# Attention products of two units issued together in one accumulator bank, with two buffers of transposed probabilities

## The reference, cut to what matters

```
h = ln(x) + shift;  qkv = h @ Wqkv.T
q, k = ln(q), ln(k)                        # per head
scores = q @ k.T / 8                       # [256, 256] per head
attn = softmax(scores);  o = attn @ v
x = x + o @ Wout.T
gate = softmax(x @ Wgate.T); each expert takes its 512 best tokens,
    applies ln, fc1, gelu, fc2, weights the result and adds it to its tokens
```

## Time and profile before

| | |
|---|---|
| time, median of 3 runs | 1130.69 us (1130.3 to 1131.01) |
| the profiled execution | 1129.59 us, span 1127.8 us |
| PE busy | 1085.8 us, 96% |
| PE weight loads busy | 859.1 us, 76% |
| DVE, ACT, POOL busy | 883.3 us, 742.6 us, 621.8 us |

### The profile page before, as it was taken

One profiled execution on the slowest core, in us unless ns is written; L12 is line 12 of the kernel. 1 busy time (PEld: TensorE's weight loads), 2 busy tenths in 40 slices (PEclk: granted clock), 3 DMA queues, 4 the chain that ended last, 5 costly groups with the idle time before them and its releaser, 6 DMA issues.

```text
span 1127.8 us, 24669 instructions
## 1 busy us (share of the span) xinstructions
PE 1085.8 (96%) x8063; PEld 859.1 (76%) x8070; DVE 883.3 (78%) x1677; ACT 742.6 (66%) x2023; POOL 621.8 (55%) x656
## 2 busy tenths in 40 slices
PE   8899999999999999999999999999988689999996
PEld 6677778778777778778787777787764258899985
DVE  5888787888888888888888888887776868777773
ACT  5777777777777777778777777777763224555441
POOL 2566566666656665666666565666671033543432
PEclk9999999999999999999999999999999999999998
DMA  5000000000001000000000010000003314544422
GB/s 187 19 11 20 19 20 19 19 19 19 19 23 32 19 19 19 19 19 19 19 19 19 19 37 19 19 10 20 11 20 142 80 35 170 141 128 112 113 30 27
DMA packets 31775, 48.62 MB, mean 43 GB/s; under 512 B 7920, under 2 KB 28528, under 8 KB 30448
## 3 DMA queue, kind: packets, MB, share of 16 engines
q1 hardware_dynamic: 25584, 39.49, 10.7%
q0 software_dynamic: 6144, 8.52, 4.1%
HBM read 35.29 MB, written 12.71 MB: 43 GB/s over the span
## 4 chain that ended last, share of the span: by engine, by line
PE 86%; DVE 6%; ACT 2%; issue 2%; POOL 1%; DMA 1%; SPq 0%; DVEq 0%; POOLq 0%; ACTq 0%
PE ch L508 14%; PE ch L509 12%; PE ch L510 12%; PE av L1699 11%; PE sc L1598 10%; PE mx L1644 9%; PE pq L1653 5%; PE ch L1715 1%; PE sc L508 1%; PE sc L510 1%; PE sc L509 1%; DVE hit L847 1%; PE ch L1615 1%; ACT prob L1174 1%; PE sc L692 1%
## 5 line engine op out<-in xcount | busy, mean ns | idle before, releaser
L1062 POOL TENSOR_TENSOR prob<-prob,inverse 128x512 f32<-128x512 f32 x254 | 260.2, 1045 | 231.6 <-DVE inverse L1402 231.6
L1174 ACT ACTIVATE prob<-sc,m 128x256 f32<-128x256 f32 x512 | 235.5, 474 | 113.5 <-DVE m L1481 110.4
L1423 DVE COPY probT<-mx 128x1024 f32<-128x1024 f32 (+1 forms) x128 | 155.2, 1213 | 57.3 <-PE mx L1644 57.3
L1481 DVE TENSOR_REDUCE m<-sc 128x4 f32<-128x1024 f32 x127 | 155.4, 1224 | 44.1 <-PE sc L1598 42.0
L1075 POOL TENSOR_TENSOR qk_lo<-qkT,qk_hi 128x512 fp32r<-128x512 f32 x128 | 171.9, 1343 | 30.4 <-ACT qk_hi L1156 30.3
L508 PE MATMUL ch<-w_hi,hT_lo 128*128 128x512 f32 x384 | 170.0, 443 | 2.5 <-DVE hT_lo L1335 2.1
L509 PE MATMUL ch<-w_lo,hT_hi 128*128 128x512 f32 x384 | 151.7, 395 | 0.0
L510 PE MATMUL ch<-w_hi,hT_hi 128*128 128x512 f32 x384 | 151.3, 394 | 0.0
L1699 PE MATMUL av<-probT,V 128*64 128x256 f32 x1024 | 138.8, 392 | 2.8 <-DVE probT L1423 2.7
L1644 PE MATMUL mx<-con,prob 128*128 128x128 f32 x1024 | 135.0, 274 | 1.9 <-POOL prob L1062 1.8
L1644 PEld LDWEIGHTS mx<-con,prob 128*128 128x128 f32 x1024 | 117.5, 140 | 16.8 <-POOL prob L1062 2.8
(11 more groups left out here) (226 smaller groups left out, 2688.0 us busy)
## 6 DMA issues: line engine op xcount, KB each, us to landing
fcw<-experts SPq DMA_DIRECT2D x8, 2048.0 KB
x_sb<-x SPq DMA_DIRECT2D x16, 256.0 KB, 2.7
xr_sb<-x SPq DMA_DIRECT2D x16, 256.0 KB, 2.8
out<-tok SPq DMA_DIRECT2D x16, 256.0 KB, 2.2
rows_dram<-xh SPq DMA_DIRECT2D x16, 256.0 KB, 2.2
prob<-w_qk SPq DMA_DIRECT2D x2, 512.0 KB, 6.7
qn<-w_qk SPq DMA_DIRECT2D x2, 512.0 KB, 7.1
V<-w_vT SPq DMA_DIRECT2D x2, 512.0 KB, 7.3
```

Of the source, the lines that this page charges most:

```text
L1062: nc.gpsimd.tensor_tensor(pr, pr, r, ALU.mult).then_inc(normalised, 1)
L1174: ins = nc.scalar.activation(prob[hp % 2][:, g * N:(g + 1) * N], sc[:, g * N:(g + 1) * N], ACT.Exp, bias=m[hp % 2][:, g:g + 1], scale=-1.0 ...
L1423: nc.vector.tensor_copy(probT[:, 0:half], mx[:, 0:half]).then_inc(probT_ready, 1)
L1481: nc.vector.tensor_reduce(m[hp % 2][:, :], sc[:, :].rearrange("p (g n) -> p g n", n=N), AX.X, ALU.min).then_inc(max_ready, 1)
```

## The change

TensorE issues the attention products only in odd steps, for two units at once: in step u (odd) those of unit u-3 into columns 0 to 255 of `av` and of unit u-2 into columns 256 to 511. `probT` has two buffers, one for even and one for odd steps. ACT's `o_hi` and DVE's `o_lo` take both units in one instruction of 512 columns, in odd steps. The waits and the projections that use `o_split` count pairs; in the drain the output projection of units 6 and 7 comes in one piece behind the last pair.

```diff
-        probT = sb("probT", [P, 2 * TT * N])
+        probT = [sb(f"probT{i}", [P, 2 * TT * N]) for i in range(2)]
...
+def pairs_done(b, hp):
+    return b * GU + (hp - 1) // 2
...
-                    if (cur and hp > 1) or (hp < 2 and prv):
-                        need(attended, u - 1)
+                    if hp % 2 and ((cur and hp > 1) or (hp < 2 and prv)):
+                        need(attended, pairs_done(b, hp))
...
-                        nc.scalar.activation(o_hi[:, (hp - 2) % UNITS, :], av[:, 0:N], ACT.Copy).then_inc(o_hi_ready, 1)
+                        pair = (hp - 3) % UNITS
+                        nc.scalar.activation(o_hi[:, pair:pair + 2, :].rearrange("p a n -> p (a n)"), av[:, :], ACT.Copy).then_inc(o_hi_ready, 1)
...
-                        need(attended, u - 2)
+                        need(attended, pairs_done(b, hp - 2 + (hp + 1) % 2))
-                        nc.vector.tensor_copy(probT[:, 0:half], mx[:, 0:half]).then_inc(probT_ready, 1)
+                        nc.vector.tensor_copy(probT[hp % 2][:, 0:half], mx[:, 0:half]).then_inc(probT_ready, 1)
...
-                        nc.vector.tensor_tensor(o_lo[:, pair, :], av[:, 0:N], o_hi[:, pair, :].bitcast(F32), ALU.subtract).then_inc(o_split, 1)
+                        nc.vector.tensor_tensor(o_lo[:, pair:pair + 2, :].rearrange("p a n -> p (a n)"), av[:, :],
+                                                o_hi[:, pair:pair + 2, :].rearrange("p a n -> p (a n)").bitcast(F32), ALU.subtract).then_inc(o_split, 1)
...
                     if drain and hp == 2:
-                        need(o_split, u - 4)
                         project(second, (5,), False)
-                        need(o_split, u - 3)
-                        project(second, (6,), False)
...
-                    if behind:
+                    if behind and hp % 2:
                         need(probT_ready, u - 1)
...
-                        need(o_split, u - 2)
+                        need(o_split, pairs_done(b, hp) - 1)
...
+                        for k in range(2):
+                            i = (hp - 3 + k) % GU
+                            gpar = ((hp - 3) % UNITS) // GU
+                            for jt in range(TT):
+                                for hh in range(2):
+                                    at = (hh * TT + jt) * N
+                                    ins = nc.tensor.matmul(av[hh * HD:(hh + 1) * HD, k * N:(k + 1) * N],
+                                                           V[gpar][:, jt, i * P + hh * HD:i * P + (hh + 1) * HD],
+                                                           probT[k][:, at:at + N], start=(jt == 0), stop=(jt == TT - 1))
                         ins.then_inc(attended, 1)
...
-                        project(second, (7,) if drain else (6, 7), True)
+                        need(o_split, pairs_done(b, 1))
+                        project(second, (6, 7), True)
```

More of the change, by code:

```diff
@@ L1131, in chunk @@
                 else:
-                    need(attended, (g - 1) * GU)
+                    need(attended, (g - 1) * (GU // 2))
                     nc.scalar.activation(V[1 if hp in ODD_STEPS else 0][:, t, :], bank[:, :], ACT.Copy).then_inc(act_read, 1)
@@ L1156, in split_high, with other_transposed @@
                     nc.scalar.activation(qk_hi[par][:, :], qkT[par][:, :], ACT.Copy).then_inc(hi_ready, 1)
-                def other_transposed(u):
+                def other_transposed(u, hp):
                     need(prob_transposed, u - 1)
-                    need(attended, u - 2)
-                    nc.scalar.activation(probT[:, 512:1024], mx[:, 512:1024], ACT.Copy).then_inc(probT_other_ready, 1)
+                    need(attended, pairs_done(b - 1, 7))
+                    nc.scalar.activation(probT[hp % 2][:, 512:1024], mx[:, 512:1024], ACT.Copy).then_inc(probT_other_ready, 1)
                 def exponentials(u, hp, first):
@@ L1218, in batch @@
                     if drain and hp < 2:
-                        other_transposed(u)
+                        other_transposed(u, hp)
                     if tail and hp == UNITS - 1:
                         exponentials(u, hp, 0)
-                    if (cur and hp > 1) or (hp < 2 and prv):
-                        need(attended, u - 1)
-                        if hp == 2 and prv:
+                    if hp % 2 and ((cur and hp > 1) or (hp < 2 and prv)):
+                        need(attended, pairs_done(b, hp))
+                        if hp == 3 and prv:
                             need(slot_filled, through("slot", b - 1, (6, 2)))
-                        if hp == 6 and prv:
+                        if hp == 7 and prv:
                             need(slot_filled, through("slot", b, (2, 0)))
-                        nc.scalar.activation(o_hi[:, (hp - 2) % UNITS, :], av[:, 0:N], ACT.Copy).then_inc(o_hi_ready, 1)
+                        pair = (hp - 3) % UNITS
+                        nc.scalar.activation(o_hi[:, pair:pair + 2, :].rearrange("p a n -> p (a n)"), av[:, :], ACT.Copy).then_inc(o_hi_ready, 1)
                     if hp == 1 and cur:
@@ L1485, in batch @@
                         split_rows(b)
-                    if (cur and hp > 1) or (hp < 2 and prv):
-                        need(o_hi_ready, u - 1)
-                        pair = (hp - 2) % UNITS
-                        nc.vector.tensor_tensor(o_lo[:, pair, :], av[:, 0:N], o_hi[:, pair, :].bitcast(F32), ALU.subtract).then_inc(o_split, 1)
+                    if hp % 2 and ((cur and hp > 1) or (hp < 2 and prv)):
+                        need(o_hi_ready, pairs_done(b, hp))
+                        pair = (hp - 3) % UNITS
+                        nc.vector.tensor_tensor(o_lo[:, pair:pair + 2, :].rearrange("p a n -> p (a n)"), av[:, :],
+                                                o_hi[:, pair:pair + 2, :].rearrange("p a n -> p (a n)").bitcast(F32), ALU.subtract).then_inc(o_split, 1)
                     if hp in (0, 3, 4, 7) and (cur if hp < 2 else nxt):
@@ L1662, in batch @@
                         second = take_bank(b, (2, 0))
-                        need(o_split, u - 4)
+                        need(o_split, pairs_done(b - 1, 7))
                         project(second, (4,), False)
                     if drain and hp == 2:
-                        need(o_split, u - 4)
                         project(second, (5,), False)
-                        need(o_split, u - 3)
-                        project(second, (6,), False)
                     elif hp == 2 and prv:
                         second = take_bank(b, (2, 0))
-                        need(o_split, u - 4)
+                        need(o_split, pairs_done(b - 1, 7))
                         if isinstance(b, int) and b == 1:
@@ L1677, in batch @@
                         first = take_bank(b, (6, 2))
-                        need(o_split, u - 4)
+                        need(o_split, pairs_done(b, 3))
                         if isinstance(b, int) and b == 0:
@@ L1689, in batch @@
                             need(probT_other_ready, hp + 1)
-                        need(o_split, u - 2)
[L1691 to L1700, removed]
+                        need(o_split, pairs_done(b, hp) - 1)
+                        if hp in (3, 7):
+                            need(act_read, through("act", b, (1, 1)) if hp == 7 else through("act", b, (0, 0)) - 1)
+                        for k in range(2):
[7 more added lines that the diff above has]
+                                                           probT[k][:, at:at + N], start=(jt == 0), stop=(jt == TT - 1))
                         ins.then_inc(attended, 1)
@@ L1718, in batch @@
                     if hp == 2 and prv:
-                        need(o_split, u - 2)
-                        project(second, (7,) if drain else (6, 7), True)
+                        need(o_split, pairs_done(b, 1))
+                        project(second, (6, 7), True)
                     if hp == 6 and cur:
-                        need(o_split, u - 2)
+                        need(o_split, pairs_done(b, 5))
                         project(first, (2, 3), True)
```

## The result

| | before | after |
|---|---|---|
| time, median | 1130.49 us (1130.2 to 1131.01, 4 runs) | 1152.61 us (1151.47 to 1154.37, 4 runs) |
| profiled execution, span | 1129.59, 1127.8 us | 1153.25, 1151.5 us |
| ratio, 95% interval | | 1.0198 (1.0186 to 1.021) |

A forecast was written before the change was run, and what follows sets the result against it. The prediction took TensorE, busy 96% of the span, as the bound. It summed 11.1 us for batches 1 to 14, 1.4 for batch 0 and 1.0 for the drain to 13.5 us slower, 1144 us; range 1135 to 1152 us.

The forecast's parts named there:

- What TensorE saves: Per pair of steps, 1.01 us leaves the even step and 0.86 us enters the odd one, saving 0.15 us.
- ACT and DVE cost nothing: Merged o_hi and o_lo save some 0.2 us per pair on each engine; neither is the bound, so costed at nothing.
- Steps 7 to 1 and 3 to 5, relief arrives whole: Transposes of steps 1 and 5: POOL's product has 2.2 us of slack, so the whole 1.01 us freed arrives.
- Step 1 to 3, "it will stand for those 1.01 us": Transposes of step 3: no slack behind POOL's product, so TensorE waits 1.01 us and none of the relief arrives.
- Step 5 to 7, 0.38 us: Transposes of step 7: slack 0.68 us, so 0.63 of the 1.01 us arrive and 0.38 us are waited for.
- The sum: One batch: 3.44 us added in odd steps, 2.65 us back in even steps, so +0.79 us.
- The ends: Batch 0 costs +1.4 us, the drain about +1 us, and the last batch's first two steps about cancel.
- ACT's and DVE's busy time fall by some 10 us: Sign expected in the profile after: the busy times of ACT and DVE fall by some 10 us.
- more waits bind: Rival, 15%: waits such as qk_lo before step 6's scores and DVE's copy in step 5 add 7 us, giving 1151 us.
- The saving arrives whole: Rival, 10%: the chain has unseen room, and 60 pairs at 0.15 us less 1 us in the drain give 1123 us.

The follow-up runs named there:

- e4: The changed kernel with o_hi and o_lo of a pair as two instructions of 256 columns each in the odd step; 1153.08 us.
- e3: The changed kernel with hT_lo in step 2 computed on 8 of its 256 columns; 1145.2 us.
- e7: The changed kernel with hT_lo of step 2 and the two xh of step 6 computed on 8 of 256 columns; 1142.38 us.
- e8: The changed kernel with DVE's two qn products of steps 2 and 6 on 64 of 512 columns, order untouched; 1122.03 us.
- e1: The changed kernel with DVE's reciprocals ahead of the two qn products in steps 2 and 6 instead of behind them; 1152.57 us.

## Why the prediction was too small

By its own steps:

- *What TensorE saves*: right. 1.01 us out of an even step and 0.86 us into an odd one, measured -1.00 and +0.85 (steps 0 and 1).
- *ACT and DVE cost nothing*: right. The merged instructions take 0.60 and 0.68 us, and undoing the merge changes nothing (e4).
- *Steps 7 to 1 and 3 to 5, relief arrives whole*: right within 0.05 us.
- *Step 1 to 3, "it will stand for those 1.01 us"*: this is the step that failed, and with it the time. The place, the releaser and the wait were right, the size was not. This term measured 1.42 us, and the first half of the transposes waited as well as the second. The forecast took the chain behind the copy of the values as rigid. But one link of it, POOL's product, keeps its 2.04 us only where DVE's products with two inputs don't start at the seam between its halves. TensorE coming sooner also made the scores sooner, and with them `m` and `hT_lo`, and these met POOL's product 0.4 us earlier. Without `hT_lo` the term is 0.93 us (1.42 - 0.49, e3).
- *Step 5 to 7, 0.38 us*: the wait of the transposes measured 0.37 us. The term as a whole is 0.58 us (1.44 - 0.86). Of the rest, 0.13 us is the attention product waiting for DVE's copy of `mx`: the two `xh` take 2.45 us for the 1.96 that they took before, since they now start right behind `m` and the short `logit`, with no `o_lo` between, and the first of them meets POOL's second half. About 0.07 us is that transposes that restart after a wait take 0.50 us to the next group instead of 0.43. Small `xh` removes 0.17 us (e7), which fits the first; for the second no run was made.
- *The sum*: 0.79 us forecast, 1.44 measured; +0.41 in steps 2 and 3, +0.20 in 6 and 7, +0.04 in 4 and 5. Without the two collisions it is 0.77 (e7), so the rest of the forecast's sum stands. With them a batch takes 53.3 us, not 52.6, and the wait of the weight loads of the transposes is 29.0 us, not about 20.
- *The ends*: batch 0 was +1.9 us. The forecast had 1.4, but its own terms, 3 × 0.86 less 1.01, give 1.57 before any wait. The last batch was +0.25 (forecast 0). The drain after:

```profile
876.22 1.95 PE L1704 MATMUL av<-probT,V 128*64 128x256 f32 x16
...
878.22 0.60 ACT L1234 ACTIVATE o_hi<-av 128x512 fp32r<-128x512 f32 x1 [2.14 <-PE av L1704]
...
878.85 0.69 DVE L1496 TENSOR_TENSOR o_lo<-av,o_hi 128x512 fp32r<-128x512 f32 x1 [2.04 <-ACT o_hi L1234]
...
879.59 0.39 PE L513 MATMUL ch<-wo_hi,o_lo 128*128 128x256 f32 x1 [0.52 <-DVE o_lo L1496]
...
881.01 0.28 PE L515 MATMUL ch<-wo_hi,o_hi 128*128 128x256 f32 x1
```

  and the last matmul of the projection in the kernel before, two behind the last row:

```profile
858.52 0.28 PE L510 MATMUL ch<-wo_hi,o_hi 128*128 128x256 f32 x1
```

  From the start of the last products to the start of that matmul it is 881.01 - 876.22 = 4.79 us, against 858.52 - 855.37 = 3.15: +1.64, of which step 0 of the drain gives 0.45 back. That is +1.2 for the +1 forecast. Behind the drain the profiled execution loses 1.5 us more where it had a granted clock of 0.50, the 1.2 GHz level (883.9 to 890.7 us; before, 862.1 to 865.5) and wins 0.4 back later; the medians do not have all of it.
- *"ACT's and DVE's busy time fall by some 10 us"*: the merged instructions save 13.3 us on ACT (38.3 for 51.6) and 9.4 on DVE (43.6 for 53.0). By the pages DVE fell by 12.3 us, but ACT by 1.6. The rows of two instructions that follow each other overlap (in e4 the first `o_hi` of a pair starts at 879.57, lasts 0.38 and is followed at 879.85), and the total counts such time once, so fewer instructions have less to lose there. That may be the reason; no run was made for it.

The rival "more waits bind" gave 1151 us, near the result, but named other waits (`qk_lo` ahead of the scores, the copy in step 5), and they did not bind: `PEld sc` waits for `qk_lo` 3.6 us over the whole span, in 5 places. The size was near for another reason. "The saving arrives whole" needs a chain 1 us shorter, as e8 has it: 1122.03 us for the 1123 worked out there.

## What to carry to other kernels

Before moving a block of the bounding engine by a microsecond, take the timeline at each place of the period and write down the slack of what must be ready next; where it is nothing, don't make the move there. Here the same edit gains in two places of four and loses in the other two, and made only where there is slack it beats both kernels. And a chain through DVE and POOL is not rigid: when its start moves, check which instructions of the other engine it will now run beside, since a shift of 0.4 us decided which of the two was stretched.

## What the runs showed of the hardware

- Which of DVE and POOL is stretched is decided by who is running when the other arrives. `hT_lo` arriving 0.19 to 0.35 us into a POOL instruction took 1.40 and 1.24 us and left POOL's 1.04 alone (it was the next one, `qk_lo`, that then took 1.73 and 1.74 us for 1.27); arriving at the seam of two POOL instructions, it took 0.68 and POOL's next took 1.53. Two engines with two such instructions each, as in e1, stretch each other in turns: 2.98 us for 1.28 and 2.50 for 2.04.
- `xh`, with one tensor and per-row factors as inputs, is held up as well: two of them took 1.96 us before and 2.45 after beside POOL. Even on 8 of 256 columns (e7) the two took 1.03 and 1.33 us there, against 0.28 us where POOL was idle. The same operation on another tile (`xh<-tok`, L1310 before) took 0.72 us for two where POOL was not in the way.
- Eight more attention matmuls in a running sequence cost 0.86 us, and entering and leaving their shape once costs 0.15 us (1.01 - 0.86).
